# A four-layer attention and FFN kernel on one core: a new order of the turns of six interleaved streams on five engines, with the blank matmuls placed anew

## The reference

```python
x = x + L0_xattn(ln(x), ctx)      # 16 heads of 16, softmax(q k^T / 4) v, then W_O
x = x + L0_ffn(ln(x))             # one of 8 experts, by the largest gate score
x = x + L1_xattn(ln(x), ctx)      # as L0, scores masked by a fixed pattern
x = x + L1_ffn(ln(x))             # a small gelu net, three coupling rounds
x = x + L2_xattn(ln(x), ctx)      # sigmoid features, linear attention
x = x + L2_ffn(ln(x))             # linear plus the two best of 8 rank-4 experts
x = x + L3_xattn(ln(x), ctx, mask)  # one head of 256
x = x + L3_ffn(ln(x))             # silu(gate) * up, down; weights dequantised from int32
```

## Time and profile before

| | |
|---|---|
| Runs | 987.82, 987.90, 988.53 us; median 987.9 |
| Span of the profiled execution | 986.1 us, 1.8 below the median of the runs; its own time outside the profiler's span is not listed |
| Instructions | 17493 |
| TensorE busy | 949.3 us, 96% of the span |
| VectorE, ScalarE, GpSimd busy | 634.1, 536.3, 221.5 us |
| Mean granted TensorE clock | 0.993 |
| Chain that ended last | TensorE 77%, ScalarE 9%, VectorE 8% |

### The profile page before, as it was taken

The page is one execution under the profiler, slowest core; times in us unless marked ns, Lnnn a source line. Parts: engine busy times, 40 slices in busy tenths (PEclk is TensorE's granted clock), DMA queues, the critical chain, the costliest instruction groups (busy, mean ns, idle before and its releaser), DMA issues.

```text
span 986.1 us, 17493 instructions
## 1 busy us (share of the span) xinstructions
PE 949.3 (96%) x6126; PEld 702.7 (71%) x6126; DVE 634.1 (64%) x2245; ACT 536.3 (54%) x1097; POOL 221.5 (22%) x317
## 2 busy tenths in 40 slices
PE   8999999989999999999999999999999999999998
PEld 6665665757687766778687766776686757777777
DVE  4634674675675776867586776775776676736564
ACT  1341644776368643875448644866376544864421
POOL 3104311303240132403141023302321032012210
PEclk9999999999999999999999999999999999999999
DMA  7308535400540023520432104402132004000000
GB/s 261 58 30 226 127 113 113 88 10 17 113 94 9 11 50 70 113 49 13 80 73 46 44 1 86 98 11 49 27 67 59 12 17 92 1 12 1 1 1 22
DMA packets 41078, 58.27 MB, mean 59 GB/s; under 512 B 4096, under 2 KB 35840, under 8 KB 37376
## 3 DMA queue, kind: packets, MB, share of 16 engines
q1 hardware_dynamic: 39600, 48.59, 23.6%
q10 hardware_dynamic: 1392, 8.56, 2.3%
HBM read 41.67 MB, written 13.89 MB: 56 GB/s over the span
## 4 chain that ended last, share of the span: by engine, by line
PE 77%; ACT 9%; DVE 8%; issue 4%; POOL 1%; DMA 1%; ACTq 0%; SPq 0%; DVEq 0%; POOLq 0%
PE bank L1657 11%; PE bank L1984 6%; PE bank L1517 6%; PE bank L1736 6%; PE bank L1714 6%; PE bank L1508 6%; PE bank L1629 4%; PE bank L1995 4%; PE bank L1771 4%; PE bank L1765 3%; PE bank L1717 3%; ACT PT L886 2%; ACT QA L873 2%; PE bank L1797 2%; PE bank L1526 2%
## 5 line engine op out<-in xcount | busy, mean ns | idle before, releaser
L886 ACT ACTIVATE PT<-bank 128x512 f32<-128x512 f32 x256 | 153.0, 598 | 127.4 <-PE bank L1717 71.8
L1657 PE MATMUL bank<-w,xhT 128*128 128x512 f32 x256 | 126.8, 599 | 0.0
L1714 PE MATMUL bank<-QA,KA 104*128 104x256 bf16 x512 | 112.7, 273 | 12.4 <-ACT PT L886 10.5
L1184 DVE CUSTOM_DVE_ANT_0 bank<-bank,maskb 128x256 f32<-128x256 f32 x256 | 101.7, 450 | 25.7 <-PE bank L1629 25.4
L1177 DVE TENSOR_REDUCE mx<-bank 128x2 f32<-128x512 f32 x128 | 83.6, 684 | 28.9 <-PE bank L1629 28.5
L1629 PE MATMUL bank<-KA,QA 96*128 96x256 bf16 x512 | 91.1, 273 | 1.9 <-DVE mx L1184 0.8
L1984 PE MATMUL bank<-xhBT,wi 128*128 128x256 f32 x336 | 87.0, 390 | 2.9 <-DVE hT L1491 2.5
L1714 PEld LDWEIGHTS bank<-QA,KA 104*128 104x128 bf16 x512 | 46.5, 99 | 60.3 <-issue 45.8
L1230 DVE SCALAR_TENSOR_TENSOR x<-bank,one,x 128x256 f32<-128x256 f32 x128 | 61.5, 481 | 21.6 <-PE bank L1657 17.6
L873 ACT COPY QA<-bank 8x256 bf16<-8x256 bf16 (+1 forms) x128 | 67.8, 575 | 10.1 <-PE bank L1695 8.8
L1984 PEld LDWEIGHTS bank<-xhBT,wi 128*128 128x128 f32 x336 | 59.2, 191 | 12.9 <-DVE hT L1491 5.6
(11 more groups left out here) (311 smaller groups left out, 2028.3 us busy)
## 6 DMA issues: line engine op xcount, KB each, us to landing
QA<-scratch SPq DMA_DIRECT2D x90, 128.0 KB, 4.8
scratch<-kparts SPq DMA_DIRECT2D x30, 192.0 KB, 2.4
KA<-scratch SPq DMA_DIRECT2D x15, 384.0 KB, 4.6
scratch<-qparts SPq DMA_DIRECT2D x30, 192.0 KB, 2.3
KA<-scratch SPq DMA_DIRECT2D x15, 256.0 KB, 5.5
w<-pack ACTq DMA_DIRECT2D x1, 2345.0 KB, 8.3
wi<-ipack ACTq DMA_DIRECT2D x1, 2304.0 KB, 8.5
xin<-x_in SPq DMA_DIRECT2D x8, 256.0 KB, 6.3
```

Source lines behind the costliest of these rows:

```text
L886: act.activation(PT[:, n % RING, :, :].rearrange("p t s -> p (t s)"), st_bank[:, :], ACT.Exp).then_inc(exp_s, 1)
L1184: last = dve.tensor_tensor_reduce(s, s, maskb[:, t, :], op0=ALU.add, op1=ALU.max, scale=1.0, scalar=-HUGE, accum_out=mx[:, i % 4, n % GH, ...
L1657: last = pe.matmul(bank[n % 2][:, :], xhT[:, kk, t * P:(t + 1) * P], W("exp0", KT)[:, kk, i * 512:(i + 1) * 512], start=(kk == 0), stop=(k ...
L1714: last = pe.matmul(st_bank[:, t * S:(t + 1) * S], KA[m][0:KM, v, t * P:(t + 1) * P], QA[m][0:KM, v, :], start=True, stop=(m == 0))
```

## The change

Only the six strings of `TURNS` change. Each stream keeps its steps, their order among themselves, their buffers and their waits; how the streams interleave on each engine is new. The counts of turns stay the same on all engines (SyncE 156, GpSimd 242, ScalarE 768, VectorE 937, TensorE 1506 working turns) but for the blank ones: w goes from 106 to 160 turns, z from 54 to 58, so TensorE gets 116 blank matmuls more (from 336 to 452).

```diff
     "vector":
-        "ppppppvppppvppppvssssssssssssssssssssvvpvpvpvspspssssssssssspssssspssssspssssbsssssssssvsssssvsspsvs"
+        "vvppppppvpppppppssspsssssssssssssssssvvpvvppvsspssssssspsssspsssssssppssssssssssssssvsbsbvpsvvspssps"
...
     "tensor":
-        "pppwwwppwwwwwwwwwwwwwwwwppwwwwwwwwwwwwpwwwwwpwpwwwwwwppwwwwwwwwwwwwwwwwwwwsswwspspssvsvswwvsvpsvswwv"
+        "ppwwwwwwwwwwwwwwwwwwwwwwwwwwwwwwwwwwwwwwwwwwwwwpwwppppwwwwwwwwwwwwwwwpwwwpwpwwwwwppwwwwwwwwwwwwwwww"
...
```

More of the change, by code:

```diff
@@ L99 @@
[L99 to L103, removed]
@@ new lines @@
+        "pppppppppppvvpvvvvvpvvvvpvvvvvvvvvvvvppssspppssvvbvppbvvpvvvvvbvpvsvvvvvvvvvvvpbpvbvvvpvvvbbbvsvvvvp"
+        "vbvvvvpbvbvbvbvvvbssapabvbapbavabvvvavpvbbvvvapavavavvvvvavvvvavaavppavvsvvvvvavvvabvvvvvvvbvvvbvpvb"
+        "vsbppsabbaavavbvavbavpvbpabvpvvvbvabpavbvvvavvvvavvvavbaaavvvvvapvavvpvvsvvbvbvvvvbvvvvvbpvbbppsasba"
+        "abvavpavpvvabvpvvbvvabvavbvvvvbvavavpavvavaaabvpvpvavavvsvvvvvpbvbvvbvvvvvvpbvpvbvbvssbapbpabavbavpb"
+        "vavvvbavpvvvvbvvavavavavbvavvvavaapvapvvvvvavsavvvvvpbvbvvvbvvvbvvvbbvvppssbababavavabvvvapvpvbvpvva"
@@ new lines @@
+    "tensor":
+        "ppwwwwwwwwwwwwwwwwwwwwwwwwwwwwwwwwwwwwwwwwwwwwwpwwppppwwwwwwwwwwwwwwwpwwwpwpwwwwwppwwwwwwwwwwwwwwwww"
+        "wwwwwwwwwwwwwwwwwwwwwwwwwwwwwwwsswwspspsvssvswvvsvsssvspvssvsvpvpvwwvvvvwwvwwwwwvvvvpvpvwwvvwwvpvwwv"
+        "wwvvpwpwwswwssssssssssssssspsspwppwwwspsspwwwsspsspsvssvbvsbbsvspvsbsvbvpvvpsvswwvsswvvvvbbvsvvssvvp"
+        "vbvpvvssvpvwwvssvsvspsvspsvswpvvspswsvwwvpvpvvsvssvssvvvvssvsvvsvvsvssvssvvssvsvsvppvvspsspassaassss"
+        "vavasssavvsvspavssvavsvasvpsvspsasaspsvvsavvsvsspvvasvvssvavavsvsavpvasvsvvpvapvsvvpsvsvssvsavvsvasv"
+        "asvvvsvvsssbvvsvvbvpvssvvsbvsvbvbpvsvpsbsbbpapssasbasbbssavpasvsbsasvvsbbpassvbvbaavbsbspsabvvsbvsps"
+        "vpbbvavbbsvvsavbsbvvbsvvbasvbvbvvassavbvbvassvsavsapvpvbsbsvvpvabvavpvavvspvsvssvvbsbvpsvspsvvsvvbss"
+        "bvbvssvvsbsvbvsbvssvvpbpbsbasspasbasspsbabvssavspspasvsvbvsbaspsvavbvbsvavsbbvpsasbvsvsbvsvasvbbvvss"
+        "pvvbsasbvsbbvabasvabvavspavpasbbvspsvvbbvpsvapvvabpvsavpvsvsvvssvsbsbvvssvssbvsbvvbvvpvpvsbvsbvbvssv"
+        "svbsvbbpvvspsspbpasbsbssaabssbsavbbasvpsbsbvaspvbsvbvsapvssbsvavpvbsvavvvbssbvsbabbbsavsbvabvpvavsbs"
+        "vbvavassvssavpsasvsvsavvpvvpvbvpvapvsavsavvsvssvbsvbvvssvssbvvbbsvvsvssvsbsbvbvsvbsbvbvpvpvvspsspbas"
+        "sbsbaasbbssavbsasvbsapvvpsvsabsvavbvpvsvsasbsbvssaspvsvssbvsvbvspvsvavsvbbasbvbvbsbsvsavavavbvsbsavv"
+        "abvabvpbsvpvvssvsvasvvavssvavvvsvvssvbvvsvbvpvssvvbsvbvbvpvvsbsbbssapababsbpasspabspsbssbsavpssbvsbs"
+        "spvsvpvsbvbsvsapvvbvbssvavvvvbbvavsspvsbbsvvsavbsvbsbassbsabbsvsvbvssbvassvbvvavavbvpsbavsvssvsssavs"
+        "asvvsvssvssvvasasvasvsvvvbbvvsvsvspvbvbvbvcvcvvcbcbbcasbsaassbbsasvasvsabsvvbbvsasvbbvavasbbvvasbbas"
+        "vsbsabvvvabvbavavvbvbvbabvbabazbvbvvbvzabvabvavvzzzzzzzzzbabaaaaazzzzaabaabaabazaaaaaaaaaabazzabaaaa"
+        "aabaaaaazzzzzzzzzzzbzzbabaaaazzazzzzbzzbbcczccbbzzzzzzbbzzzzzzbcbcccbbzzzzzzbcbcccbccccbbbbcbccccccc"
+        "cccccccccccccccccccccccc",
```

50 lines of the change are left out of this document (17 added, 33 removed).

## The result

The changed kernel takes **1032.0 us** (median of four runs, 1030.7 to 1035.6), the kernel before 987.9: a ratio of 1.046, interval 1.043 to 1.048. It is slower, as forecast, but by 44 us where 14 were forecast, outside the range. The profiled execution has a span of 1029.1 us against 986.1 before, 43 more.

A forecast was written before the change was run, and what follows sets the result against it. TensorE's queue, busy 949.3 of 986.1 us, was taken to bound the kernel. The start's 9.8 - 2.0 + 6.3 = 14.1 us, with 0 for the rest, on 987.9 gave 1002.0 us; forecast 997 to 1008, range 992 to 1012.

The forecast's parts named there:

- Step 1: VectorE, start: both KA fills precede batch 0's norm; xh0 comes at 14.6 instead of 8.5, hidden behind blank matmuls.
- Step 2: TensorE, before the turning of xh0: 90 blank matmuls at 0.109 us each make it 9.8 us late, at 20.2.
- Step 3: ScalarE and the queries' split on VectorE: 2.0 of 9.8 us given back; L1535 starts at 30.3, 7.8 us late.
- Step 4: `third(0)`, held by VectorE and ScalarE in turn: fewer blank matmuls and the missing fill gain nothing; L1560 at 38.0.
- Step 5: TensorE, before the first scores: 96 blank matmuls, 58 more than before, finish last and cost 6.3 us, unhidden.
- Sum of the start: Up to the first scores: 9.8 - 2.0 + 6.3 = 14.1 us, first scores at 49.4 instead of 35.3.
- The rest: I take 0: Behind the first scores: counts of neighbouring turns show a weave of the same kind, so 0 us.
- upper bound, 9.5: Behind the first scores, worst case: TensorE's idle time from 250 to 900 us doubles, plus 9.5 us.
- The clock: I book nothing: TensorE: ending clock dips could return at most 4.6 us, but the clock was already whole at the added blanks; 0.
- The rest gets worse too: Behind the first scores: clock or new waits, such as a VectorE step too early, cost 6 to 15 us; chance 0.18.
- The new weave earns more: Behind the first scores: gaps of the exponential's round trip get filled, each up to 0.9 us, outweighing the start; chance 0.07.
- idle time from 265 to 915 still 9 to 12 us: Sign for the profile after: TensorE's idle time behind the first scores stays at 9 to 12 us.

The follow-up runs named there:

- e4: The kernel before with only VectorE's two KA fills moved ahead of the first norm: 992.9 us (1.006).
- e3: The changed kernel with 42 instead of 90 blank matmuls before the turning of xh0 and 30 instead of 96 before the first scores: 1022.3 us (1.036).
- e1: The kernel before with the changed order on every engine up to the first scores, old order behind them: 1007.5 us (1.021).
- e2: The kernel before with the old order up to the first scores and the changed order behind them: 1017.2 us (1.030).
- e6: Old start, changed order behind it, GpSimd's splits shrunk to 8 of 256 columns per half from the second batch on: 993.1 us (1.006).
- e5: The kernel before with GpSimd's splits shrunk to 8 of 256 columns per half from the second batch on: 981.9 us (0.994).
- e15: The whole change with GpSimd's splits shrunk to 8 of 256 columns per half from the second batch on: 1013.6 us (1.026).
- e11: e6 with three 128x512 GpSimd instructions on spare tiles, awaited by nobody, added behind each split's signal: 1022.0 us (1.035).
- e10: e5 with three 128x512 GpSimd instructions on spare tiles, awaited by nobody, added behind each split's signal: 996.1 us (1.008).
- e7: e2 with two TensorE turns of the coupled net moved three or four turns later, at one long wait for VectorE: 1018.3 us (1.031).
- e9: e2 with each 128x512 split of GpSimd written as two of 128x256, nothing left out: 1011.1 us (1.024).
- e13: The kernel before with all long GpSimd instructions (splits, sums with a bias, x + xh) shrunk to 8 columns: 979.6 us (0.993).
- e14: e2 with all long GpSimd instructions (splits, sums with a bias, x + xh) shrunk to 8 columns: 988.0 us (1.000).

## Why the prediction was right in sign and wrong in size

- **Step 1, the fills first: right.** VectorE's two fills end at 10.8, xh0 is there at 13.8, 0.8 earlier than said since the weights came that much sooner, and it is hidden as said. Uncovered, and with the clock's dip that came along, it cost 4.7 us in e4.
- **Step 2, 90 blank matmuls: right.** 9.83 us from first to next, 0.109 each; the turning starts right behind.
- **Step 3: right.** L1536 at 29.50, 30.4 without the head start of 0.9, where 30.3 was said; it waits for vaug, 1.96 us.
- **Step 4: 1.5 us too low.** L1561 is at 38.64, 39.5 without the head start, where 38.0 was said. TensorE's clock stood at the lower level for 3.4 us from 32.9 on, and L1553 took 2.08 us where L1560, of the same shape, takes 1.13. The prediction had no term for it.
- **Step 5, 96 blank matmuls on the path: right.** 10.48 us to the scores, no idle time before them. e3 prices both runs: 9.7 us.
- Sum of the start: said 14.1, measured 14.8 at the first scores, or 15.7 without the head start: two misses, step 4 and the early weights, partly cancel, and that is luck. e1 ran the start alone, at 20, of which some 5 are clock and small waits behind it.
- **"The rest: I take 0": this step failed.** The step took the count of neighbouring turns for the price of the new interleaving, and found none. It measured 28.9 us by the landmarks (43.7 less 14.8), and 30 with the old start (e2). Its upper bound, 9.5, was no bound: it doubled the idle time of one stretch and said nothing of the other engines' own durations. The count of neighbouring turns found "no side is better" because it looked at one engine's list at a time. What decides for the most part is which VectorE instruction runs while GpSimd runs a long one. Shrinking the splits took 18 of the 29 us between the orders away with the old start (11.2 left between e6 and e5) and 16 of 29 in the whole change (12.5 left between e15 and e5), and load that nobody awaits brought the distance back to 26 (e11, e10). Some 8 of the 29 us are left with all long GpSimd instructions shrunk, and their cause is open.
- **"The clock: I book nothing": wrong, but second.** 38 us at the lower level instead of 14; the two stretches looked at begin behind waits (210.4 to 227.5 us behind a row of waits for ScalarE and VectorE from 199 on, 442.5 to 446 behind the wait of 3.55 us). At half pace 24 us more cost 12 us at most. Between two executions of the changed kernel a mean clock 0.009 lower went with 4.8 us more (0.983 and 1028.9 us, 0.974 and 1033.7), which would make the difference to before, 0.011, worth some 6. No run kept TensorE busy through its waits, so this share is argued, not shown.
- **The rivals.** "The rest gets worse too" named the right engine, VectorE, and new waits behind the first scores, with 0.18 and 6 to 15 us; its sign was right, its size a fifth to a half. Its mechanism, a step too early in VectorE's own list, is not what the runs show: the steps are held up by GpSimd. "The new weave earns more" has nothing for it.
- Of the signs named in advance, idle time from 265 to 915 still 9 to 12 us is the one that failed: 19.0 us from 265 to 930.

## What to carry to other kernels

When an order of work is exchanged, each engine's list can look alike and the pairs across engines not: read durations of the same instruction in different places of the old trace, and ask which neighbour on another engine ran beside the slow ones. In this kernel a small `tensor_scalar` or `scalar_tensor_tensor` of VectorE on SBUF beside 1.16 us GpSimd instructions took about a microsecond, so a tuned order can owe part of its time to keeping them apart. Halving such GpSimd instructions gave 0.35% with nothing moved; quarters were slower than wholes. A run of blank matmuls placed for a wait must be sized by that wait, since here what was over stood on TensorE's path until the next wait took its place (9.7 us for 114 of them).

## What the runs showed of the hardware

- Beside GpSimd's 128x512 instructions L1313 and L1314 took 1.0 to 1.2 us instead of 0.17 to 0.29, L1318 0.72 to 1.32 instead of 0.35. Not every VectorE instruction is held up, and to touch only SBUF is not enough. In the nine runs with whole instructions of GpSimd (before, the change, e1 to e4, e7, e10, e11), the TENSOR_SCALAR, SCALAR_TENSOR_TENSOR, TENSOR_TENSOR, CAST and COPY on SBUF tiles were (but for cbase, 128x1, 0.21 us in 9 cases); mq's TENSOR_SCALAR (L1197), for one, had a median of 0.40 us in the 72 cases beside an instruction of over 0.9 us, 0.17 otherwise. BATCH_NORM_STATS2 (0.41 us in 36 cases for bst_p, longest 0.42), RECIPROCAL and TENSOR_REDUCE read and write only SBUF too and were as long beside GpSimd as without it. So were those with an operand in PSUM: L1178 (128x512) had a median of 0.68 us beside a long GpSimd instruction (39 of them in the changed kernel) and 0.68 without (89). In the changed kernel (times in ns: shortest, median, longest):

```profile
L1065 DVE BATCH_NORM_STATS2 bst_p<-xin x16: 407/414/427, 10.8 to 667.6; 128x6 f32<-128x256 f32 x16
L1178 DVE TENSOR_REDUCE mx<-bank x128: 656/683/694, 50.5 to 788.2; 128x2 f32<-128x512 f32 x128
L1198 DVE SCALAR_TENSOR_TENSOR mq<-mx,mq x64: 170/171/1153, 53.9 to 906.5; 128x8 bf16<-128x8 f32 x64
```

- The Trainium skill (SBUF — State Buffer, "SBUF: two separate sides") says that GpSimd shares a pair of SBUF ports with those VectorE instructions that run in a 2-port mode or have two SBUF inputs, as "an exclusive lock, not a bandwidth split", held for the whole instruction by whichever starts first. The trace agrees: a held instruction ends shortly behind a GpSimd instruction's end, halves (e9) hold up less than wholes, and only some kinds of instruction are held. In which mode an instruction ran, the trace does not show.
- The price shows neither as GpSimd's time (220.8 against 221.5 us) nor as idle time of VectorE, but as VectorE's busy time: 643.6 instead of 634.1 us. With all of GpSimd's long instructions shrunk it is 617.1 in the old order (e13) and 614.4 in the order of e2 (e14), so the hold-ups were there before the change as well, some 17 us of them, and went to some 30.
- The same start came out 2.4 us (e1) and 3.3 us (e15) later than in the changed kernel, each time with TensorE's clock at the lower level for 10 and 7 us between 30 and 41 us, where the change had 3.4. A wait of 2 us for vaug stands just before in all three; why the clock then differed is not shown.
- Open: what the remaining 8 us between the orders are made of, waits or the clock behind them. A run that fills TensorE's waits at 189 to 198 us with blank matmuls would tell for that place; it was not tried.
